# Score tiles that wait one by one, and the product with V in two halves

## The reference, cut to what matters

```python
q = (x @ Wq + bq).reshape(Bn, Nn, H, d)     # H = 16, d = 16, Nn = 2048
k = (x @ Wk + bk).reshape(Bn, Nn, H, d)
v = (x @ Wv + bv).reshape(Bn, Nn, H, d)
scores = jnp.einsum('bnhd,bmhd->bnmh', q, k) / math.sqrt(d)
att = jax.nn.softmax(scores, axis=2)
attval = jnp.einsum('bnmh,bmhd->bnhd', att, v).reshape(Bn, Nn, Dn)
```

## Time and profile before

| | us |
|---|---|
| median of 3 runs | 1253.62 |
| lowest, highest | 1252.13, 1257.34 |
| the profiled execution | 1257.07 |
| its span, first to last instruction | 1255.3 |

### The profile page before, as it was taken

One profiled execution on the slowest core, in us unless ns is written; L12 is line 12 of the kernel. 1 busy time (PEld: TensorE's weight loads), 2 busy tenths in 40 slices (PEclk: granted clock), 3 DMA queues, 4 the chain that ended last, 5 costly groups with the idle time before them and its releaser, 6 DMA issues.

```text
span 1255.3 us, 17929 instructions
## 1 busy us (share of the span) xinstructions
PE 1058.8 (84%) x6130; PEld 516.6 (41%) x6130; DVE 903.6 (72%) x1113; ACT 690.4 (55%) x1253; POOL 245.1 (20%) x284
## 2 busy tenths in 40 slices
PE   4888888888878888887888878888999999999995
PEld 3433222222222222222222222222447778888874
DVE  5458788788785887886788878876647686656665
ACT  0212577777775777776777777777663232232321
POOL 1123844000000100400000000301213050232323
PEclk9869699999996999998999999999889999999997
DMA  7796000020000000000000000002110000000001
GB/s 174 191 135 137 28 14 2 14 72 1 14 14 1 14 1 14 14 1 15 1 14 15 1 14 14 1 1 66 51 51 1 17 1 1 18 1 1 17 0 34
DMA packets 27557, 36.72 MB, mean 29 GB/s; under 512 B 5632, under 2 KB 18528, under 8 KB 26720
## 3 DMA queue, kind: packets, MB, share of 16 engines
q1 hardware_dynamic: 24256, 34.12, 11.5%
q10 hardware_dynamic: 3232, 1.60, 0.6%
HBM read 24.70 MB, written 10.49 MB: 28 GB/s over the span
## 4 chain that ended last, share of the span: by engine, by line
PE 73%; ACT 14%; DVE 5%; issue 4%; DMA 1%; ACTq 1%; SPq 0%; POOL 0%; DVEq 0%; POOLq 0%
PE ps L575 21%; PE ps L546 19%; ACT prob L1027 12%; PE ps L711 11%; PE ps L510 6%; PE ps L699 6%; PE ps L450 2%; DVE mxp L1249 1%; PE ps L461 1%; DMA kst<-k_parts 1%; PE ps L639 1%; PE ps L870 1%; PE ps L841 1%; PE ps L568 1%; PE ps L617 1%
## 5 line engine op out<-in xcount | busy, mean ns | idle before, releaser
L1249 DVE TENSOR_REDUCE mxp<-ps 128x2 f32<-128x1024 f32 x512 | 620.9, 1225 | 178.0 <-PE ps L510 170.3
L1027 ACT ACTIVATE prob<-ps 128x512 f32<-128x512 f32 x1024 | 553.9, 596 | 215.3 <-PE ps L546 192.6
L546 PE MATMUL ps<-qst,kst 50*128 50x512 f32 x1024 | 263.1, 513 | 143.1 <-ACT prob L1027 122.6
L575 PE MATMUL ps<-prob,vp 128*32 128x512 f32 x2048 | 285.4, 631 | 0.0
L546 PEld LDWEIGHTS ps<-qst,kst 50*128 50x128 f32 x1024 | 98.6, 190 | 453.8 <-ACT prob L1027 413.4
L510 PE MATMUL ps<-kst,qst 48*128 48x512 f32 x1024 | 215.1, 419 | 14.5 <-DVE mxp L1249 8.5
L510 PEld LDWEIGHTS ps<-kst,qst 48*128 48x128 f32 x1024 | 101.9, 196 | 37.6 <-DVE mxp L1249 22.8
L1062 ACT ACTIVATE hid_hi<-hid 128x512 fp32r<-128x512 f32 (+1 forms) x56 | 35.4, 632 | 132.4 <-DVE hid L1401 103.1
L1731 POOL TENSOR_TENSOR att_u<-o_tm,rec 128x256 f32<-128x256 f32 x16 | 9.9, 620 | 413.6 <-DVE rec L1258 413.5
L575 PEld LDWEIGHTS ps<-prob,vp 128*32 128x32 f32 x2048 | 40.9, 109 | 97.4 <-issue 97.1
L1396 DVE SCALAR_TENSOR_TENSOR hid<-ps,bu,sig 128x512 f32<-128x512 f32 (+1 forms) x56 | 41.8, 746 | 48.2 <-PE ps L711 38.3
(11 more groups left out here) (211 smaller groups left out, 1081.4 us busy)
## 6 DMA issues: line engine op xcount, KB each, us to landing
qst<-q_parts SPq DMA_DIRECT2D x96, 64.0 KB, 2.3
kst<-k_parts SPq DMA_DIRECT2D x24, 256.0 KB, 14.1
k_parts<-parts SPq DMA_DIRECT2D x8, 512.0 KB, 3.1
q_parts<-parts SPq DMA_DIRECT2D x8, 512.0 KB, 2.8
x<-x SPq DMA_DIRECT2D x4, 512.0 KB, 9.3
wmod_sb<-wmod ACTq DMA_DIRECT2D x3, 512.0 KB, 9.0
wmod_sb<-wmod SPq DMA_DIRECT2D x1, 1536.0 KB, 6.9
out<-x SPq DMA_DIRECT2D x3, 512.0 KB, 2.9
```

Of the source, the lines that this page charges most:

```text
L546: last = nc.tensor.matmul(ps[:, two_banks[b], :], kst[rows, GP * g + a, P * t:P * (t + 1)], qst[rows, g, a, :], start=True, stop=True)
L575: last = nc.tensor.matmul(ps[VW * k:VW * (k + 1), 7, :], vp[:, t, G * g + k, :], prob[:, t % 2, k, :], start=t == 0, stop=t == MT - 1)
L1027: nc.scalar.activation(prob[:, t % 2, k, :], ps[:, banks[(G * t + k) % len(banks)], :], ACT.Exp, scale=DH ** -0.5).then_inc(p_s, 1)
L1249: nc.vector.tensor_reduce(own, ps[:, 2 * p:2 * p + 2, :], AX.X, ALU.max).then_inc(mx_read, 1)
```

## The change

- Each of the four score tiles of a step waits for its own bank and reports by itself (`sc_ps` counts 4 a step, not 2; all that wait for it count likewise). ScalarE waits before every head.
- The order of a step becomes: tiles 0 and 1, `maxima` p = 0, tile 2, half of `weigh` (256 queries), tile 3, `maxima` p = 1, the other half of `weigh`. In step 4 `maxima` p = 0 stands behind the first half of `weigh`.
- `weigh` of a step is eight products of 256 queries instead of four of 512. It has a wait of its own for the exponentials of the step before.

```diff
-                    for a in range(GP):
-                        n = G * t + 2 * a
-                        two_banks = [banks[(n + b) % len(banks)] for b in range(2)]
-                        turn_max = a == 1 and t == TURN_MAX and ahead >= 1
...
-                        if n + 1 >= len(banks):
-                            pe.wait_ge(p_s, u * (G * MT) + n + 1 - len(banks) + 1)
...
+                    def score(k):
+                        n = G * t + k
+                        bank = banks[n % len(banks)]
+                        turn_max = k == 2 and t == TURN_MAX and ahead >= 1
+                        if n >= len(banks):
                             pe.wait_ge(p_s, u * (G * MT) + n - len(banks) + 1)
...
+                        if turn_max:
+                            max_row(u + 1, bank)
+                            pe.wait_ge(nmT_s, u + 2)
+                        rows = slice(HALF * (k % 2), HALF * (k % 2) + KR + NM)
+                        nc.tensor.matmul(ps[:, bank, :], kst[rows, GP * g + k // 2, P * t:P * (t + 1)],
+                                         qst[rows, g, k // 2, :], start=True, stop=True).then_inc(sc_ps, 1)
...
+                    def weigh_before(half):
+                        if t == 0 and not first:
+                            weigh((g - 1) % NG, MT - 1, half)
+                        if t >= 1:
+                            pe.wait_ge(p_s, u * (G * MT) + G * t)
+                            if t == 1 and half == 0 and not first:
+                                pe.wait_ge(o_s, u)
+                            weigh(g, t - 1, half)
+
+                    score(0)
+                    score(1)
+                    if not late:
+                        next_maxima(0)
+                    score(2)
+                    weigh_before(0)
+                    if late:
+                        next_maxima(0)
+                    score(3)
+                    next_maxima(1)
+                    weigh_before(1)
...
-            def weigh(g, t):
+            def weigh(g, t, half):
+                cols = slice(CH // 2 * half, CH // 2 * (half + 1))
                 for k in range(G):
-                    last = nc.tensor.matmul(ps[VW * k:VW * (k + 1), 7, :], vp[:, t, G * g + k, :], prob[:, t % 2, k, :],
-                                            start=t == 0, stop=t == MT - 1)
-                last.then_inc(pv_s, 1)
+                    last = nc.tensor.matmul(ps[VW * k:VW * (k + 1), 7, cols], vp[:, t, G * g + k, :], prob[:, t % 2, k, cols],
+                                            start=t == 0 and half == 0, stop=t == MT - 1 and half == 1, skip_group_check=True)
+                if half == 1:
+                    last.then_inc(pv_s, 1)
...
-                        if k % 2 == 0:
-                            act.wait_ge(sc_ps, u * (GP * MT) + GP * t + k // 2 + 1)
+                        act.wait_ge(sc_ps, u * (G * MT) + G * t + k + 1)
```

More of the change, by code:

```diff
@@ L374, in _ @@
                     stored(sp, range(len(ITEMS) - SLOTS, len(ITEMS)))
-                sp.wait_ge(sc_ps, GP * MT * (v - NG + 1))
+                sp.wait_ge(sc_ps, G * MT * (v - NG + 1))
                 load_q(g, c)
@@ L385, in _ @@
             store_max(NG - 1)
-            sp.wait_ge(sc_ps, GP * MT * (NU - 2))
+            sp.wait_ge(sc_ps, G * MT * (NU - 2))
             load_gate_up(wu_raw, up_w, su_w, ffw_in[1])
-            sp.wait_ge(sc_ps, GP * MT * (NU - 1))
+            sp.wait_ge(sc_ps, G * MT * (NU - 1))
             sp.dma_start(wd_raw[:, 0:IE, :], down_w.rearrange("e i d -> (e i) d").rearrange("(t p) d -> p t d", p=P)
@@ L531, in unit @@
                     late = t == 4 and not first
-                    for a in range(GP):
-                        n = G * t + 2 * a
-                        two_banks = [banks[(n + b) % len(banks)] for b in range(2)]
-                        turn_max = a == 1 and t == TURN_MAX and ahead >= 1
-                        if turn_max:
+                    def score(k):
[3 more added lines that the diff above has]
+                        if n >= len(banks):
@@ L537, in unit @@
                             pe.wait_ge(p_s, u * (G * MT) + n - len(banks) + 1)
-                            max_row(u + 1, two_banks[0])
-                            pe.wait_ge(nmT_s, u + 2)
-                        if n + 1 >= len(banks):
-                            pe.wait_ge(p_s, u * (G * MT) + n + 1 - len(banks) + 1)
                         elif n == 0 and not first:
                             pe.wait_ge(p_s, u * (G * MT))
[L544 to L553, removed]
-                            maxima(vg, i, p, pairs + p)
[L556 to L561, removed]
+                        if turn_max:
+                            max_row(u + 1, bank)
+                            pe.wait_ge(nmT_s, u + 2)
@@ new lines, in score, with next_maxima @@
+                        rows = slice(HALF * (k % 2), HALF * (k % 2) + KR + NM)
+                        nc.tensor.matmul(ps[:, bank, :], kst[rows, GP * g + k // 2, P * t:P * (t + 1)],
+                                         qst[rows, g, k // 2, :], start=True, stop=True).then_inc(sc_ps, 1)
+                    def next_maxima(p):
+                        if run:
+                            if late and p == 0:
+                                pe.wait_ge(oT_s, u)
+                            maxima(vg, i, p, pairs + p)
@@ L721, in _ @@
             pe.wait_ge(p_s, NU * G * MT)
-            weigh(NG - 1, MT - 1)
+            for half in range(2):
+                weigh(NG - 1, MT - 1, half)
             hidden((wg_hi, wg_lo), 0, 0, 1).then_inc(g_ps, 1)
@@ L1800, in _ @@
                 if u == NU - NG:
-                    pool.wait_ge(sc_ps, GP * MT * (NU - NG + 1))
+                    pool.wait_ge(sc_ps, G * MT * (NU - NG + 1))
                     gate_rest()
@@ L1819, in _ @@
             deviation(1, NC - 1)
-            pool.wait_ge(sc_ps, GP * MT * NU)
+            pool.wait_ge(sc_ps, G * MT * NU)
             input_rest(NC - 1)
```

## The result

| | before | after |
|---|---|---|
| median, us | 1252.88 (4 runs) | 1713.54 (4 runs, 1700.41 to 1717.96) |
| span of the profiled execution | 1255.3 | 1708.7 |
| mean granted clock of TensorE | 0.950 | 0.618 |

The ratio is 1.366 (95% interval 1.357 to 1.375). I had forecast 1227, in a range of 1200 to 1258.

A forecast was written before the change was run, and what follows sets the result against it. It took the order of a step, TensorE and ScalarE taking turns, as the bound. Eleven ordinary units at -2.71 gave -29.8; with -2, -2 and +7, -26.8: 1257.07 to 1230.3, or 1227 us from the median; range 1200 to 1258.

The forecast's parts named there:

- Other units: Units outside the eleven ordinary ones: 12 or 13 low-clock steps, 4.77 for 4.5 each; changes of -2, -2 and +7 us.
- The loop through ScalarE: Attention's second pass: tiles 2 and 3 wait for exponential 0, setting the 2.93 us round; the change would remove this.
- TensorE's own work, 2.71: Sum of TensorE's pieces in a step of the new order, 2.71 us against a round of 2.93; 2.74 with waits.
- The lost pairing: In a step, tile 2 streams alone, giving five streaming slots of 0.22 us where there were four.
- The 0.11 of a change of shape: Cost in us of TensorE going from row halves to weigh's column strips; four changes a step instead of two.
- The 0.03 for the waits: Three more register waits a step on TensorE, bounds 0 to 0.24 us, taken as 0.03.
- Step 12: Step whose tile behind max_row waits for ScalarE's copy, starting 1.97 us after the first tile; costs 0.70 more a unit.
- Rival A: VectorE becomes the bound at 2.54 to 2.6 us a step; about 1194 us; chance 0.10.
- Rivals C and D: C: extra waits cost 0.08 each, about 1268 us. D: tiles 0 and 1 stop pairing, same time. Together 0.14.
- the 7 for unit 15: Last unit, steps without maxima: TensorE's step goes from 1.68 to 2.25 us, about 12 steps, 7 us lost.

The follow-up runs named there:

- e5: Changed kernel with ten float32 products of 128 by 512 put in step 3 of unit 0, into bank 0; 1689.58 us.
- e10: e5 with both halves of the product with V moved ahead of tile 2 in step 12; 1295.46 us.
- e2: Changed kernel with the product with V whole (512 queries), in one place between tiles 2 and 3; 1215.44 us, ratio 0.970.
- e14: Changed kernel with only the second half of the product with V moved, directly behind the first; 1201.55 us, ratio 0.963.
- e4: Kernel before, order kept with whole product with V last; only the score tiles' waits and reports taken apart; 1284.42 us.
- e11: e10 with the ten products also in step 2 of units 1, 5, 9 and 13; 1270.28 us, ratio 1.016.
- e8: Changed kernel with one product more a step: that of maxima 1 on rows 64 to 111 also issued beside tile 2; 1404.35 us.
- e7: Kernel before, without the second product of maxima 1 (rows 64 to 111) inside the units; 1363.85 us.
- e13: Changed kernel with only step 12 altered: both halves of the product with V back to back ahead of tile 2, no burst; 1322.72 us.
- e12: e2 plus one tiny product a step between tile 1 and maxima 0, forcing two more changes of shape; 1389.87 us.
- e6: Changed kernel with the two products of maxima 1 parted, one beside tile 2 and one beside tile 3; 1304.72 us.
- e3: Kernel before with the product with V in two halves of 256 queries back to back, nothing else; 1253.19 us, ratio 1.000.

## Why the prediction was wrong

The failed step is the one headed "Other units". There I read two long intervals and a low clock in the earlier trace rows, counted "some 12 or 13 steps in all" at the lower level and carried that count over unchanged. It became all 16 units. I worked out the cost of a step at that level (4.77; measured 4.74, as I had entered 0.45 for a slot of 0.43), but not that the length of such a spell depends on the very order that the change rewrites. By my estimate, 78.32 against the 45.9 that I had forecast for a unit (48.63 - 2.71) makes 32.4, and 15 units of it the whole miss of 486 us. I named no rival for it, though the chain of my own argument had the entry: unit 0 began at the lower level, and something had to lift it.

The rest, by its steps:

- The loop through ScalarE goes: right. ScalarE's share of the chain fell to 1%, and `e5` shows steps on end without a stall before L545 at the upper clock too.
- TensorE's own work, 2.71, and 2.74 with the waits: right, 2.70. The lost pairing and the half of `weigh` at 0.57 (144.07 to 144.64) stand in the rows of `e5`. The 0.11 of a change of shape fits them, but it is worked out (0.33 less a stream of 0.22), and no row shows it by itself, as the prediction's "The trace shows" has it. `e5` measures unit 0, whose waits compare with constants; inside the loop, where the value stands in a register, a step of `e10` takes 2.69 (227.16 to 229.85). The 0.03 for the waits was too much.
- Step 12 costs more now: right in place, the tile behind `max_row` starts 1.81 after the first of its step (167.42 to 169.23) for my 1.97. What I did not see is that at this gap the clock falls in the new order, as it did not before.
- Rival A had VectorE as the bound at 2.54 to 2.60. `e2` and `e14`, with two changes of shape, come near that number, 2.60 and 2.61, but not by that mechanism: in both VectorE stands still for 0.24 to 0.26 of a step.
- Rivals C and D: waits that cost, pairs that part. Neither. Tiles 0 and 1 start as a pair (603.97 x2), and `e4` has the step of before.
- Had the clock held, the forecast was near: `e11`, with 5 bursts and 99 us at the low level left, ran 1270, and its ordinary units take 44.4, with step 12 filled. No run held the clock with step 12 as the change has it, so the 0.70 that I charged for it is not measured, nor is the 7 for unit 15.

What is shown: the second half's place alone makes 1713 or 1202 (`e14`); more rows in use at the same busy time and order bring the clock back (`e8`); fewer delay it (`e7`); five of five returns follow the two halves standing together (`e10`, `e13`); in the new order the clock falls right behind a gap of 0.86 (`e5`), and with that gap filled and the halves together it does not fall there (`e10`). What stays open: by what measure the clock comes back. Neither the mean over a step (`e12` came back with less, `e4` came back later with the same) nor one dense stretch (`e12` came back late, `e10` and `e13` each passed a step 12 by, and `e6` and `e8` came back with the halves apart) explains all the delays by itself. `e14` does not part the place of the half from the two changes of shape that go with it. Chance may have a share: `e5` to `e8`, `e10`, `e12` and `e13` are single executions and don't show how much these delays vary.

## What to carry to other kernels

When TensorE starts a stage at 1.2 GHz, ask of a new order not only what a step costs at each level but what in it would lift the clock; a spell's length read from the old kernel is not a constant. Be wary of work that runs alone in half of the array's rows, and of dense products broken up between such work: here the two together kept a TensorE that was busy for 49.35 of 50 us at half speed through a whole stage. If a change makes everything of one engine in one stage longer, look at the granted clock first, and try the dense products together.

## What I had not expected of the hardware

- TensorE was busy for 49.35 of 50 us at a granted clock of 0.50 and stayed there for 1263 us; the same products with one half moved ran at 1.00, but for spells of 10 to 17 us in the attention (`e14`).
- Eight products of 256 columns back to back take the same 1.00 as four of 512 (`e3`).
- At the upper clock a gap of 0.86 us was followed by the lower level in one order (`e5`), while before stands still for 1.03 in the same step and keeps it.
- One more product a step, on rows that stood idle, cost no time at the lower clock (4.75 with and without) and brought the upper one back (`e8`).
